# A relational graph layer: a group's first tile behind one unit of matmuls, its other tiles behind the next

## The reference

```python
h = maximum(layernorm(x), 0)
u = h @ root + bias
for r in range(8):
    mask = (edge_type == r)
    sums = segment_sum(h[src] * mask, dst, 1250)      # over the edges of this type
    cnt = segment_sum(mask, dst, 1250)
    u = u + (sums / maximum(cnt, 1)) @ weight[r]
z = concatenate([u, h]) @ w_gate + b_gate
out = x + tanh(u) * z + h * (1 - z)
```

## Time and profile before

| | us |
|---|---|
| median of 3 runs | 1519.31 |
| lowest and highest | 1516.27, 1519.83 |
| profiled execution | 1518.65 |
| its span, first to last instruction | 1516.9 |

### The profile page before, as it was taken

The page is one execution under the profiler, slowest core; times in us unless marked ns, Lnnn a source line. Parts: engine busy times, 40 slices in busy tenths (PEclk is TensorE's granted clock), DMA queues, the critical chain, the costliest instruction groups (busy, mean ns, idle before and its releaser), DMA issues.

```text
span 1516.9 us, 20122 instructions
## 1 busy us (share of the span) xinstructions
PE 1311.0 (86%) x6165; PEld 655.7 (43%) x6165; DVE 939.5 (62%) x1328; ACT 408.9 (27%) x501; POOL 732.7 (48%) x994
## 2 busy tenths in 40 slices
PE   3979997999998498988887999997887789977798
PEld 1434443444443244444443444443443344434465
DVE  6677686476656355753555667665544557684776
ACT  5442231232324113221222143232201213433000
POOL 2412007787878566665635547543656465320000
PEclk9999998999999799999998999999999989989899
DMA  5632141252234277766754774774676857664886
GB/s 204 212 135 78 53 158 37 49 165 51 62 107 133 76 231 244 218 176 218 221 160 139 264 225 147 254 229 128 191 244 201 273 166 212 225 197 134 212 221 185
DMA packets 108104, 259.15 MB, mean 171 GB/s; under 512 B 20826, under 2 KB 21329, under 8 KB 108020
## 3 DMA queue, kind: packets, MB, share of 16 engines
q1 hardware_dynamic: 75204, 175.63, 35.7%
q0 software_dynamic: 32816, 82.39, 19.6%
HBM read 194.34 MB, written 82.17 MB: 182 GB/s over the span
## 4 chain that ended last, share of the span: by engine, by line
PE 27%; DMA 24%; POOL 19%; issue 13%; DVE 10%; ACT 3%; SPq 2%; POOLq 1%; DVEq 0%; ACTq 0%
PE ps L1272 22%; DMA early<-y_rows,idx 18%; POOL table_rows L571 15%; PE ps L1233 5%; DMA out_dram<-hT 3%; POOL onehot L605 2%; DVE W L900 2%; DMA y_rows<-yhl 1%; POOL early L597 1%; DMA hT<-u_rows 1%; DVE hT L948 1%; DVE hT L953 1%; POOL dcol L586 1%; ACT early L689 1%; DMA W<-in_L_gnn_weight_dram 1%
## 5 line engine op out<-in xcount | busy, mean ns | idle before, releaser
L1272 PE MATMUL ps<-W,hT 128*128 128x512 f16 (+2 forms) x4860 | 1100.9, 387 | 24.4 <-DVE W L900 23.3
L1272 PEld LDWEIGHTS ps<-W,hT 128*128 128x128 f16 (+2 forms) x4860 | 499.7, 104 | 581.5 <-issue 52.4
L1233 PE MATMUL ps<-early,onehot 128*125 x768 | 208.4, 409 | 107.4 <-POOL onehot L605 97.3
L571 POOL DMA_INDIRECT table_rows<-edge_src,table_i x160 | 225.9, 1412 | 146.2 <-DVE table_i L973 89.4
L597 POOL DMA_INDIRECT early<-y_rows,idx x192 | 222.7, 1160 | 118.0 <-PE ps L1236 70.3
L605 POOL TENSOR_SCALAR onehot<-iota_d,dcol 128x125 f16<-128x125 f16 x184 | 153.2, 833 | 210.7 <-DMA early<-y_rows,idx 207.2
L729 ACT ACTIVATE yhl<-W 128x512 f16<-128x512 f32 x120 | 75.3, 628 | 444.3 <-DVE W L1024 242.3
L1233 PEld LDWEIGHTS ps<-early,onehot 128*125 x768 | 103.8, 143 | 173.7 <-issue 130.3
L900 DVE SCALAR_TENSOR_TENSOR W<-W,wsc 128x2048 f16<-128x2048 f32 x65 | 153.2, 2361 | 25.9 <-ACT W L679 21.0
L679 ACT ACTIVATE W<-W,wsc 128x2048 f16<-128x2048 f32 x65 | 128.2, 1989 | 16.9 <-DVE W L916 11.8
L648 ACT ACTIVATE peek_out<-W 128x1024 bf16<-128x1024 f32 x84 | 88.4, 1052 | 95.6 <-DMA W<-in_L_gnn_weight_dram 74.7
(11 more groups left out here) (162 smaller groups left out, 715.4 us busy)
## 6 DMA issues: line engine op xcount, KB each, us to landing
y_rows<-yhl SPq DMA_DIRECT2D x144, 256.0 KB
W<-in_L_gnn_weight_dram SPq DMA_DIRECT2D x32, 1024.0 KB
early<-u_rows SPq DMA_DIRECT2D x40, 448.0 KB
u_rows<-early SPq DMA_DIRECT2D x40, 448.0 KB
W<-in_L_gnn_w_gate_dram SPq DMA_DIRECT2D x8, 1024.0 KB
early<-in_x_dram SPq DMA_DIRECT2D x9, 512.0 KB, 4.4
hs_rows<-early SPq DMA_DIRECT2D x9, 512.0 KB, 2.9
u_rows<-yhl SPq DMA_DIRECT2D x18, 256.0 KB
```

The source lines that it names most:

```text
L571: pool.indirect_dma_start(out=table_rows, out_offset=bass.IndirectOffsetOnAxis(ap=at_i[:, c:c + 1], axis=0), in_=packed[0:EP, c:c + 1], in ...
L1233: nc.tensor.matmul(ps[0:DT, 4 + half, :], hot_t, rows[:, bass.ds(ring_slot * (2 * D) + (half * D + part * HC), HC)], start=first and part ...
L1272: last = nc.tensor.matmul(ps[0:rows, n % 4, :], hT[:, m, v_h, k, n0:n0 + rows], Wh[:, MAT[w][c], v_w, k, :], start=(first and v_h + v_w == ...
```

## The change

`REST_AT[g]` is new: the unit behind which TensorE does the second and later tiles of a group. It is one more than `AGG_AT[g]` where the next group is at least two units off and the sweep isn't the third, else the same. So 59 groups are split: 30 in the first sweep, 20 in the second, nine in the last. VectorE's addition, the end of a step and all that hangs on it (store and load of the accumulator tile, scaling, turning) follow `REST_AT`. The last group of the last sweep stays whole behind unit 298. The weight maximum of the gate's second half, which may not fall among the matmuls of a turn, moves from unit 297 to 298.

```diff
+    REST_AT = [AGG_AT[g] + (1 if g + 1 < NG and AGG_AT[g + 1] >= AGG_AT[g] + 2 and group(g)[0] != 2 else 0) for g in range(NG)]
...
-    STEP_END = [AGG_AT[SPAN[s][0] + (j + 1) * (SWEEPS[s][1] - SWEEPS[s][0]) - 1] for s, j in STEPS]
+    STEP_END = [REST_AT[SPAN[s][0] + (j + 1) * (SWEEPS[s][1] - SWEEPS[s][0]) - 1] for s, j in STEPS]
...
-    SCALE_AT[W_GU] = FIRST[W_GH] + 27
+    SCALE_AT[W_GU] = next(n for n in range(FIRST[W_GH] + 26, FIRST[W_GU]) if n not in TURN_U and n + 1 not in TURN_U)
...
-                for g in AGG.get(n - 1, ()):
+                for g in REST.get(n - 1, ()):
                     add_group(g)
...
-            def sum_group(g):
+            def sum_first(g):
                 t0 = pe.value_load(bounds[0:1, g:g + 1], min_val=0, max_val=TMAX - RING)
-                t1 = pe.value_load(bounds[0:1, g + 1:g + 2], min_val=2, max_val=TMAX)
                 if g:
                     pe.wait_ge(s["u_added"], g)
                 else:
                     pe.wait_ge(s["table_ready"], 1)
                 sum_tile(t0, True)
+
+            def sum_rest(g):
+                t0 = pe.value_load(bounds[0:1, g:g + 1], min_val=0, max_val=TMAX - RING)
+                t1 = pe.value_load(bounds[0:1, g + 1:g + 2], min_val=2, max_val=TMAX)
                 with pe.Fori(t0 + 1, t1) as t:
                     sum_tile(t, False)
...
-                for g in AGG.get(n, ()):
-                    sum_group(g)
+                for g in range(NG):
+                    if AGG_AT[g] == n:
+                        sum_first(g)
+                    if REST_AT[g] == n:
+                        sum_rest(g)
```

More of the change, by code:

```diff
@@ L125, in gated_rgcn_preln @@
     assert all(AGG_AT[g] >= FIRST[W_OF[SWEEPS[group(g)[0]][1] - 1] + 1] + 3 for g in range(NG)) and AGG_AT == sorted(AGG_AT)
-    AGG = {}
+    REST_AT = [AGG_AT[g] + (1 if g + 1 < NG and AGG_AT[g + 1] >= AGG_AT[g] + 2 and group(g)[0] != 2 else 0) for g in range(NG)]
+    AGG, REST = {}, {}
     for g in range(NG):
         AGG.setdefault(AGG_AT[g], []).append(g)
+        REST.setdefault(REST_AT[g], []).append(g)
     STEPS = [(s, j) for s in range(NS) for j in range(NJ)]
-    STEP_END = [AGG_AT[SPAN[s][0] + (j + 1) * (SWEEPS[s][1] - SWEEPS[s][0]) - 1] for s, j in STEPS]
+    STEP_END = [REST_AT[SPAN[s][0] + (j + 1) * (SWEEPS[s][1] - SWEEPS[s][0]) - 1] for s, j in STEPS]
     FINAL = (NS - 1) * NJ
```

## The result

The changed kernel takes 1507.85 us (median of 7 runs, 1499.86 to 1513.53), the kernel before 1519.31 us (median of 7 in the same comparison). The ratio is 0.9929, with a 95% interval of 0.9902 to 0.9956: 10.8 us faster, 7 to 15 us by the interval. The forecast of 1507 us is met, and by luck: as the experiments show, one term of its sum was about twice as large as predicted and paid for another that was nothing. The profiled execution took 1508.55 us with a span of 1506.8 us, against 1516.9 us before. All helper lines stand 4 to 7 lines lower in the changed kernel (L1237 and L1240 are the tile's matmuls, L609 the one-hot, L1105 the addition).

The account below looks back on a forecast made before the run. TensorE sets the pace in some stretches, the supply of gathered tiles in others. Gains of 2 + 4.2 + 0.5 + 5 = 11.7 us off the profiled 1518.65 us gave 1507 us, range 1499 to 1518.

Parts of the forecast that it names:

- Supply and TensorE: First sweep: the supply of gathered tiles runs at its own speed, so a TensorE that is early merely waits longer.
- the waits simply go: Rival: the waits vanish, 27.3 us of them in the first sweep; 48 us faster, 1470 us; chance 0.04.
- Term 1: First sweep: later tiles one unit later cover late one-hots, less new waits for additions; -3 to +5 us, taken as 2.
- Eight places: First sweep: eight units where VectorE converts or sums weights bring waits for additions, 0.5 to 2.5 us each, 12 in all.
- a sign of being wrong: The prediction is wrong if TensorE's new waits for additions run above 12 us.
- gathers end at most 4 us earlier: First sweep: sign in the changed kernel's profile that its gathers end at most 4 us earlier.
- The slower rival: Additions become the new bound and new waits can lower TensorE's clock; 7 us lost, 1526 us; chance 0.10.
- Term 2: Two changes of sweep: accumulator store and load go behind the last product store; gain 4.2 us, between 3 and 5.
- passes through whole: Changes of sweep: the 4.2 us gain reaches TensorE in full, as it waits about 8.15 us for each first one-hot.
- Term 3: Second sweep: 0.85 us of waits for one-hots are left to win; gain taken as 0.5 us.
- Term 4: Last sweep: waits fall, above all VectorE's 5.0 us for an accumulator load; bounds 0 and 10 us, taken as 5.
- The extra loads: Each split group adds one load of a bound into a register, hidden behind a unit's matmuls; cost taken as 0.

Follow-up runs that it names:

- e12: Kernel before with its first two sweeps one unit later and the third sweep two units later, nothing split: ratio 0.9911.
- e3: Changed kernel with only 29 of the 30 groups of the first sweep split, its change of sweep not touched: ratio 0.9975.
- e2: Kernel before with only the accumulator's store and load put behind the last product store at the two changes of sweep: ratio 0.9929.
- e11: Kernel before with its first two sweeps three units later, nothing split: ratio 0.9866.
- e4: Changed kernel with only the nine groups of the last sweep split: ratio 1.0054.
- e7: Changed kernel with the first two sweeps split and the last sweep as before: ratio 0.9928.
- e5: Changed kernel's code with no group split and nothing later, only its form with loads of its own: ratio 1.0030.
- The halved pair: Whole groups one unit later, and the changed kernel, both with gathers fetching half of each row: ratios 0.9650 and 0.9707, medians 1463.5 and 1475.3 us.
- e1: Changed kernel with no group split, whole groups standing behind the later unit: ratio 0.9872, median 1504.6 us.
- e6: Kernel before with its first two sweeps one unit later, nothing split: ratio 0.9877, median 1498.1 us.

## Why the prediction was right in its number and wrong in its sum

- **Supply and TensorE** (the reading of the earlier trace rows): right. A TensorE that is earlier waits longer, as in e12's third sweep. The rival "the waits simply go", 1470 us, fell with it. What the reading left out is that GpSimd's own steps are stretched beside VectorE's sums and conversions, 18.8 us in the first sweep's one-hots.
- **Term 1, the first sweep, gain 2.** The mechanism was right and both sizes were off. Eight places were named and priced at 0.5 to 2.5 us, 12 in all. Eight waits for additions came, 15.4 us in all, 3.4 the longest, but only six of them at the named places (behind units 103, 107, 117, 126, 128 and 138). None came behind 142 and 147, and two came that weren't on the list: 0.55 us behind 151 and 2.16 us behind 161, directly behind tile 68, where the prediction had the whole cover of 2.6 us count. The 15.4 us are above the 12 us which the prediction had called a sign of being wrong. Waits for one-hots fell to 11.0 us, where 10 or less was forecast. What the sweep gained can't be read from one trace: with the same order of work its last tile ended at 787.3, 788.8, 791.6, 792.5 and 797.6 us in five kernels, and the changed kernel's 786.5, one unit (2.6 us) further on, is 7.6 us ahead of their mean, against a spread of 10. By time, e3's 0.9975 makes it 3.8 us, between a loss of 0.6 and a gain of 8.2, and e3 also carries the form's price in the sweeps that it doesn't split. The 2 us are neither shown nor refuted. The sign "gathers end at most 4 us earlier" (3.5 us seen) tests nothing, for the same reason.
- **The clock.** The slower rival's premise, that new waits of this size mostly leave it high, was taken from a wait of 1.81 us. The same trace has one of 1.87 us, at 583.61, behind which a tile took 1.53 us in place of 1.05 and two units 6.54 in place of 5.34. In the changed kernel three of the five above 2 us lowered it, 1.7 us each, 5 us in all, which no term held.
- **Term 2, the changes of sweep, 4.2.** Right in place and cause, mis-sized by half: 9.0 us in the queue for the two, 7.4 us in the changed kernel's first waits, and by e2 as much as the whole measured gain (10.8 us, 6 to 15 by the interval). The step that failed is "4.3 us, less some 0.1": it counted the issue alone. The prediction had left open in a sentence that "if the transfers ahead had held the store back as well, more would be won"; they had, by 2.5 us at the first change. The rows before gave a hint: from the store's issue at 802.25 to GpSimd's going on at 807.15 are 4.9 us, for a store of 98 rows, while the same page has 2.9 us in the median from issue to landing for a store of 512 KB. That the gain "passes through whole" failed in part: at the first change against e2, 2.1 us of it went into the long one-hot beside VectorE's work. The last product store was issued as forecast, within 0.35 us of VectorE's end.
- What the Trainium skill says in Trainium Kernel Development and Optimization, Key Constraints, that DMAs share 16 engines and interleave, is no contradiction to this, but the prediction's reading of it, that only the issue time is won (2.1 us a change), is. The runs show 4.5 us: what stands ahead in the same queue delayed the store beyond the issue. After the move the same bytes, issued 0.05 us behind it, did not: GpSimd goes on 2.68 to 2.77 us behind VectorE, as it does at 2.72 in e11, where no such transfer follows for 3 us. Here the order in the queue mattered, not the sharing.
- **Term 3, 0.5:** below what any run here can tell.
- **Term 4, the last sweep, 5.** Wrong. VectorE's wait for the load did go, as forecast, and bought nothing: waits for additions (8.7 for 3.2 us) and for turned tiles (11.3 for 5.2 us) took its place. The step that failed treated VectorE as the loaded engine and asked only what it waits for; the split makes TensorE wait for the same VectorE one unit sooner, the very cost that term 1 had counted and term 4 left out. By e4, 1.0054 (1.0021 to 1.0088), there is no gain; e7 alone can't tell 5 us.
- **The extra loads, 0.** Right for split groups. For those left whole, the prediction had said nothing: there both bounds are loaded behind the first tile, up to 1.57 us in the open, and the form cost 0.3% (0.01 to 0.59%) in e5, where no group is split.
- **The slower rival** (additions bind): it was real and not large enough. The halved pair shows 9 to 16 us where whole groups would have been the alternative; against the kernel before, what was lost to it was covered by term 2.

What stays open: how e1 and e6 gain some 8 us more by time than e2 does. Both have its two changes of sweep and a first sweep one unit later; their last first-sweep tile ends at 790.8 and 790.9 us with one unit more done, 3 us ahead of the mean at an equal point, well inside the spread. e12, whose order is e6's up to there, ended that sweep at 783.1, 7.8 us earlier. No run isolates the gain from this scatter. Nor is it settled why e4 lost 8 us by time, when 0.7 us lie in its last sweep and its form costs some 5, or how much the supply would gain if GpSimd's steps didn't fall beside VectorE's.

## What to carry to other kernels

Before a phase that waits for a store, look at what stands ahead of that store in its queue: here a store and a load that nobody needed for several units cost 4.5 us each time, twice what their issue took, and moving them alone gave as much as the whole change. When work depends on a late supply, try moving it later as a whole before splitting it: here that did at least as well, and left the accumulator's hand-over its distance. Take a delay from the first thing that its end releases; one step further on it may be mixed with another engine's work. Price a moved dependency in every stage that it passes through, not only in the one where you first found it, and expect no gain from taking a wait away from an engine whose partner then comes earlier.

## What the runs showed of the hardware

With the same order of work, the first sweep ended up to 10 us apart in five kernels (787.3 to 797.6 us), while the time from VectorE's last product row to GpSimd's going on came out within 0.1 us in sixteen cases (2.68 to 2.77 us). Effects of the first kind need many runs, those of the second one trace. A transfer behind two others in the same queue was known to be done 7.2 us behind VectorE's end, behind one 4.8 and behind none 2.7. GpSimd's copy of 0.18 us took 1.80 to 1.89 us in all sixteen cases, ending where VectorE's pair of sums ended, and 0.18 us in nine of the ten cases in which it came behind them; in the tenth, beside a conversion, it took 2.33. Some of the loads of a register before a matmul lay open for 0.9 to 1.6 us in e5, and most are not seen.
